# A fused attention, dense, SwiGLU and adapter kernel: SyncE's and GpSimd's orders in the first group, repeated waits of ScalarE, and the order at the end of attention

## The chip, the cores and the metric

One NeuronCore of one Trainium2 chip runs one program. The metric is the time of an execution on the device, in microseconds. The kernel before took 1306.64 us (median of three runs, 1304.0 to 1306.82).

## What is computed

Four residual steps on x, of shape [8, 128, 512] in float32:

```python
x = x + attention(x, Wq, Wk, Wv, Wo, norms, k_cache[block_table], v_cache[block_table], seqlens)
x = x + (x @ W.T + b) + coeff[b] * (x @ (2*mask[b] - 1))      # dense, its weights differ by batch element
x = x + down(silu(gate(x)) * up(x))                            # with low-rank adapters chosen by index
x = x + x @ weight[ids[b]].T
```

Attention has 8 batch elements, 8 key heads with 4 query heads each, head size 128, and 640 keys for each query: 512 out of 16 cache pages and 128 new ones. Queries and keys pass an RMS norm and a rotation by position.

## The kernel before

TensorE multiplies every float32 pair in three passes: each operand is split into a high part (a rounded copy, made by ScalarE) and a low part (the difference, made by GpSimd or VectorE), and `three_pass` (L65 to L67) issues high by high, high by low and low by high.

The work of attention is ordered as 8 groups (one per key head, `g`) of 8 rounds (one per batch element, `b`). Groups 1 to 6 are one loop on each engine; group 0, group 7 and `ending` (the last two rounds) are written out. Each engine's order within a round is written by hand, and semaphores carry all dependences. In round b an engine works on three elements at once: b (probabilities turned and multiplied with the values), the next one `(g1, b1)` (scores, softmax) and the one after that `(g2, b2)` (projection, rotation). A pass over one element goes so:

- TensorE projects the queries; VectorE multiplies them with cosines and sines (`turn_q`); GpSimd combines the halves (`rotate_q`, L568 and L569); VectorE transposes 32 by 32 squares (`spread_queries`, L1114); SyncE writes them to a scratch tensor in HBM with four DMAs (`store_queries`, L415, tensor `q_rows`) and reads them back transposed with one (`read_queries`, L421, tile `at_qT_raw`), a round later.
- ScalarE makes their high part (`queries`, tile `ds_lo`, L758) and GpSimd their low part (`queries`, L618). TensorE then forms the scores of four heads, VectorE masks them and takes the maximum (`mask_and_max`, L1073), ScalarE exponentiates (`exps`, L810), VectorE inverts the row sums (L1079, L1083), and GpSimd multiplies (`normalise`, L628).
- Three of the five chunks of probabilities are turned on TensorE (L1353); the other two go through HBM (`store_turned`, L402, then `read_turned`, L408, four DMAs, tensor `turned_rows`).

The cache has to be brought into page order for each key head. In group 0 the keys of elements 0 to 3 and all values come by row gathers that GpSimd issues (`gather`, L524). Meanwhile the pages of the next group are copied through one staging tile, `kv_stage`: GpSimd gathers 1 MB into it (`stage_pages`, L556, one step in each of four rounds), SyncE waits for that (`kv_staged`) and stores it in HBM (`store_pages`, L397, `kT_pages` and `v_pages`). GpSimd's next step waits for that store (`kv_stored`). `load_keys` (L379) and `load_values` (L385) read the pages of an element two rounds ahead.

In group 0, SyncE's round is: `read_queries`, `load_keys` where due, `store_turned`, `read_turned`, `load_x`, `store_queries`, and last `store_pages(g, b - 2)` in rounds 2 to 5. In groups 1 to 6, `store_pages(g, b - 2)` stands behind `store_turned` instead, and the steps are staged a round earlier (rounds 1 to 4), so that a step is stored a round after it is staged.

GpSimd's round in group 0 is: the row gathers for b2, `cached_keys` (L613), `queries` (L618), `rotate_q`, `key_scale`, `cached_values` (L624), the staging step, `normalise` of head 0, `query_scale` (L583, L585), `normalise` of the other heads, `rotate_k`, and `table(b + 3)` (L593).

In `ending`, the dense weights of batch elements 1 to 3 are formed on VectorE (`dense.weights`, L1564) and split (`part_hi`, L1590, ScalarE; `part_lo`, L1595, GpSimd) between the steps of the last two attention rounds. y is element 6 and z is element 7.

Of the kernel before, what the change touches and what calls it, by code (L numbers as in the profile page):

```python
# [84 lines left out]
def attention(nc, block, x, xT, ints, floats, wq, wkv, wo, k_cache, kT_cache, v_cache, kT_pages, v_pages, ident, xres, wq_raw, shared, dense, loads, turned_rows, q_rows):  # L85
# [3 lines left out]
    with ExitStack() as ctx:  # L89
# [250 lines left out]
        def _(sp):  # L340
# [89 lines left out]
            def group(g, last):  # L430
                for b in range(B):
# [17 lines left out]
                    if not (last and b >= B - 2) and not by_row(g2):  # L449
# [4 lines left out]
                    if by_moves(g, b):  # L454
                        store_turned(g, b)
                    if not by_row(g) and not last and 2 <= b < 6:
                        store_pages(g, b - 2)
                    if not (last and b >= B - 2) and not by_row(g2):
                        wait_apart(sp, v_cache_done, upto(g, b, 1, 1), passed)
                        load_values(g2, b2)  # L460
# [17 lines left out]
                    if by_row(g) and b < B - 2:  # L478
                        sp.wait_ge(xT_done, b + 3)
                        load_x(b + 2)  # L480
# [4 lines left out]
                    if by_row(g):  # L485
                        if b == 0:
                            store_first_keys(0)
                        elif 2 <= b < 6:
                            store_pages(g, b - 2)
                    elif not last and b == 0:  # L490
# [22 lines left out]
        def _(pool):  # L513
# [141 lines left out]
            def group(g, first, last):  # L655
                for b in range(B - 2 if last else B):
# [13 lines left out]
                    if b == B - 3 and not last:  # L670
                        qkv_group(g + 1, DC)
                    if keys_by_row(g2, b2):
# [5 lines left out]
                    if started:  # L678
                        if not keys_by_row(g1, b1):
                            cached_keys(g1, b1)  # L680
                        queries(g1, b1)
                    rotate_q(g2, b2)
                    if started:
                        key_scale(g2, b2)
                        cached_values(g1, b1)
                        stage()
                    else:
                        rotate_k(g2, b2)
# [8 lines left out]
                    if first and b == 1:  # L697
                        stage_first_keys(1)
                    normalise(g1, b1, 0)
                    if started:  # L700
# [3 lines left out]
                    if started:  # L704
                        rotate_k(g2, b2)
                    if first and b < B - 3:
                        table(b + 3)
                    if not started:
                        query_scale(g2, b2)
# [37 lines left out]
        def _(act):  # L747
# [12 lines left out]
            def qkv_group(g, n, first=False):  # L760
                cs = slice(2 * (n - DC), 2 * (n - DC) + 2)
                out, src = (wqT_hi[:, n, :], wq_raw[:, n, :]) if n < DC else (wkvT_hi[:, cs, :], wkv_raw[:, cs, :])
                if not first:
                    act.wait_ge(q_in_psum if n < DC else kv_in_psum, g * B)
                if first and n < DC:
                    hi(out, src, (wq_half_loaded, staging_loaded)[n // 2], 16, wq_hi_done)
                else:
# [1718 lines left out]
```

## Time and profile before

| | |
|---|---|
| median of three runs | 1306.64 us |
| the profiled execution's own time | 1306.46 us |
| its span, first to last instruction | 1304.5 us |
| TensorE busy | 1274.6 us (98%), mean granted clock 0.996 |
| VectorE busy | 1015.0 us (78%) |
| GpSimd busy | 931.9 us (71%) |
| ScalarE busy | 840.0 us (64%) |

PE is TensorE's matmuls, PEld its weight loads, DVE VectorE, ACT ScalarE, POOL GpSimd, SP SyncE, whose row "SPq" is the issuing of a DMA. In a timeline a row is one or several like instructions with start, duration, what it writes and reads, and in brackets the idle time before it with what ended it. A wait is counted only where the engine was idle. A row of windows gives the stretch, its length, the busy time (and number of instructions) of PE, PEld, DVE, ACT and POOL, the granted clock as a share of 2.4 GHz, the busy share of the DMA engines and GB/s. A row of waits gives who waited, for whom, the total, the number of times and the longest. Matmuls overlap their neighbours, so that busy TensorE time is not time at full rate. Group 0 lasts to about 174 us, and attention to about 1047 us.

### The profile page before, as it was taken

To read this page: it belongs to the slowest core of one execution; us is meant where nothing else is said; L and a number is where in the kernel's file an instruction comes from. 1 tells how busy PE (TensorE), PEld (TensorE's weight loads), DVE (VectorE), ACT (ScalarE), POOL (GpSimd) and SP (SyncE) were. 2 spreads that over 40 slices of the span, in tenths; PEclk is the share of its full clock that TensorE was granted. 3 is DMA by queue.
4 is the path that set the end of the run, shared out by engine and by line. 5 is a ranking of instruction groups with operands and counts; after the bars stand their busy time and mean duration, and the time that the engine had idled before them with its cause. 6 is when DMAs were issued, how large, how long until landed. Compare 5 with 4: busy or idle time off the path is not lost.

```text
span 1304.5 us, 25321 instructions
## 1 busy us (share of the span) xinstructions
PE 1274.6 (98%) x7068; PEld 1112.4 (85%) x7068; DVE 1015.0 (78%) x2054; ACT 840.0 (64%) x2217; POOL 931.9 (71%) x1173
## 2 busy tenths in 40 slices
PE   9898999999999999999999999999999899999999
PEld 8777888888888888888888888888888788888887
DVE  6876788887887888788877887888888896748546
ACT  7665666766675767666766676676766684545444
POOL 7888887878887888787888888888887732414111
PEclk9999999999999999999999999999999999999999
DMA  6787769957985797689769966995756364354532
GB/s 224 234 243 233 208 202 275 268 142 206 275 248 161 219 284 215 176 234 278 198 177 263 259 174 181 287 274 147 232 156 170 120 193 142 131 197 135 182 127 80
DMA packets 260052, 265.86 MB, mean 204 GB/s; under 512 B 139776, under 2 KB 211072, under 8 KB 249216
## 3 DMA queue, kind: packets, MB, share of 16 engines
q1 hardware_dynamic: 254208, 228.77, 61.1%
q0 software_dynamic: 5760, 36.18, 8.2%
q8 instruction: 28, 0.46, 0.1%
q14 instruction: 56, 0.46, 0.1%
HBM read 182.57 MB, written 82.31 MB: 203 GB/s over the span
## 4 chain that ended last, share of the span: by engine, by line
PE 79%; POOL 5%; DMA 4%; DVE 4%; issue 4%; ACT 3%; SPq 1%; ACTq 0%; DVEq 0%; POOLq 0%
PE ps L65 24%; PE ps L66 23%; PE ps L67 23%; PE ps L1353 5%; DVE at_pT_lo L1021 1%; DMA shared<-in_kT_cache,at_page_idx 1%; DMA turned_rows<-at_turned 1%; DMA q_rows<-at_q_turned_rows 1%; POOL ds_lo L618 1%; POOL at_probs L628 1%; ACT at_probs L810 1%; PE ps L2308 1%; DVE xres L1090 1%; DMA at_qT_raw<-q_rows 1%; POOL at_q_rot L569 0%
## 5 line engine op out<-in xcount | busy, mean ns | idle before, releaser
L810 ACT ACTIVATE at_probs<-at_probs,at_neg_max 128x640 f32<-128x640 f32 x256 | 210.2, 823 | 122.2 <-DVE at_neg_max L1073 122.2
L628 POOL TENSOR_SCALAR at_probs<-at_probs,at_row_inv 128x640 f32<-128x640 f32 x256 | 212.9, 842 | 103.0 <-DVE at_row_inv L1083 99.5
L1073 DVE CUSTOM_DVE_ANT_0 at_probs<-ps,at_mask,at_inv_rms 128x640 f32<-128x640 f32 x256 | 223.4, 880 | 19.7 <-PE ps L67 17.3
L65 PE MATMUL ps<-ds_hi,x_hi 128*128 128x512 f32 (+1 forms) x564 | 192.8, 342 | 0.8 <-DVE x_lo L1614 0.4
L67 PE MATMUL ps<-ds_hi,x_lo 128*128 128x512 f32 (+1 forms) x564 | 192.2, 341 | 0.0
L65 PE MATMUL ps<-at_kT_hi,ds_lo 128*128 128x320 f32 x512 | 161.6, 316 | 11.4 <-DVE at_pT_lo L1021 8.5
L67 PE MATMUL ps<-at_kT_hi,ds_lo 128*128 128x320 f32 x512 | 159.7, 312 | 0.0
L66 PE MATMUL ps<-at_kT_lo,ds_lo 128*128 128x320 f32 x512 | 159.7, 312 | 0.0
L758 ACT ACTIVATE at_pT_hi<-ps 128x512 fp32r<-128x512 f32 x196 | 111.4, 604 | 69.0 <-PE ps L1353 64.6
L1021 DVE TENSOR_TENSOR at_pT_lo<-ps,at_pT_hi 128x512 fp32r<-128x512 f32 x196 | 128.5, 683 | 29.1 <-ACT at_pT_hi L758 28.4
L65 PE MATMUL ps<-at_pT_hi,at_v_hi 128*128 128x512 f32 x320 | 128.1, 400 | 8.2 <-DVE xres L1090 6.3
L66 PE MATMUL ps<-at_pT_lo,at_v_hi 128*128 128x512 f32 x320 | 126.1, 394 | 0.0
L67 PE MATMUL ps<-at_pT_hi,at_v_lo 128*128 128x512 f32 x320 | 125.0, 391 | 0.0
L1108 DVE STREAM_TRANSPOSE at_turned<-at_probs 128x768 f32<-128x768 f32 x62 | 60.7, 978 | 81.9 <-POOL at_probs L628 81.9
L66 PE MATMUL ps<-ds_lo,x_hi 128*128 128x512 f32 x308 | 120.1, 390 | 0.0
L65 PEld LDWEIGHTS ps<-ds_hi,x_hi 128*128 128x128 f32 x564 | 105.9, 188 | 16.2 <-issue 0.9
L67 PEld LDWEIGHTS ps<-ds_hi,x_lo 128*128 128x128 f32 x564 | 106.9, 190 | 12.3
L65 PEld LDWEIGHTS ps<-at_kT_hi,ds_lo 128*128 128x128 f32 x512 | 97.5, 190 | 22.9 <-DVE at_pT_lo L1021 12.6
L758 ACT ACTIVATE at_pT_hi<-at_pT_raw 128x512 fp32r<-128x512 f32 x124 | 74.9, 625 | 52.7 <-DMA at_pT_raw<-turned_rows 30.3
L65 PE MATMUL ps<-at_woT_hi,at_oT_hi 128*128 128x512 f32 x256 | 106.5, 416 | 0.0
L66 PEld LDWEIGHTS ps<-at_kT_lo,ds_lo 128*128 128x128 f32 x512 | 97.5, 190 | 4.1
L67 PE MATMUL ps<-at_woT_hi,at_oT_lo 128*128 128x512 f32 x256 | 100.7, 393 | 0.0
(226 smaller groups left out, 3624.1 us busy)
## 6 DMA issues: line engine op xcount, KB each, us to landing
turned_rows<-at_turned SPq DMA_DIRECT2D x62, 512.0 KB, 2.8
at_pT_raw<-turned_rows SPq DMA_DIRECT2D x248, 128.0 KB, 4.7
kT_pages<-shared SPq DMA_DIRECT2D x16, 1024.0 KB, 5.6
q_rows<-at_q_turned_rows SPq DMA_DIRECT2D x248, 64.0 KB, 2.9
at_qT_raw<-q_rows SPq DMA_DIRECT2D x62, 256.0 KB, 3.5
kv_raw<-kT_pages SPq DMA_DIRECT2D x60, 256.0 KB, 4.1
v_pages<-shared SPq DMA_DIRECT2D x14, 1024.0 KB, 5.7
kv_raw<-v_pages SPq DMA_DIRECT2D x56, 256.0 KB, 3.4
```

The costliest lines, as they stand in the source:

```text
L65: pe.matmul(out, l_hi, r_hi, start=first, stop=False)
L66: pe.matmul(out, l_hi, r_lo, start=False, stop=False)
L67: return pe.matmul(out, l_lo, r_hi, start=False, stop=last)
L618: pool.tensor_tensor(l, qT_raw[:].rearrange("p a h r -> p h a r"), h.bitcast(F32), ALU.subtract).then_inc(qT_done, 1)
L628: pool.tensor_scalar(probs[:, h, :], probs[:, h, :], row_inv[:, h:h + 1], 1.0, ALU.mult, ALU.mult).then_inc(probs_done, 1)
L758: act.activation(out, src, ACT.Copy).then_inc(done, 1)
L810: act.activation(probs[:, h, :], probs[:, h, :], ACT.Exp, bias=neg_max[:, h:h + 1], scale=-1.0, accum_out=row_sum[:, h:h + 1]).then_inc(ex ...
L1021: dve.tensor_tensor(out, src, hi_part.bitcast(F32), ALU.subtract).then_inc(done, 1)
L1073: dve.tensor_tensor_reduce(out=probs[:, h, :], in0=slot(h), in1=mask[:, b, :], scale=inv_rms[b % 2][:, h:h + 1], scalar=3.0e38, op0=ALU.ad ...
L1090: dve.tensor_tensor(xres[:, b, :], bank(y_bank(b)), xres[:, b, :], ALU.add).then_inc(dense.x1_ready if last else y_added, 1)
L1108: dve.transpose(turned[:, :, :, 0:n, :].rearrange("p k c h r -> p h c k r"), probs[:, 0:n, (KC - MOVED) * P:KEYS].rearrange("p h (c k i) - ...
L1353: return pe.transpose(bank(probs_bank(b, c))[:, h * S:(h + 1) * S], probs[:, h, c * P:(c + 1) * P], ident[:])
```

## The change

It reorders and removes; no arithmetic is changed.

- SyncE, group 0: `store_pages` stands behind `store_turned` and runs in rounds 3 to 6; `load_x` stands behind `store_queries`; the first load of keys and values of group 1 waits for the last page store behind `store_queries` of round 6.
- GpSimd: the row gathers and the staging step stand behind the low parts and `rotate_q`; in the round before `ending`, `query_scale` stands behind the other heads' `normalise` and `rotate_k`; in round 0 of group 0, `query_scale` stands before `table`.
- ScalarE: waits that an earlier wait of the engine already covers are taken out (`pv_done` before the high parts of the values, and the second to fourth wait of each group of weights).
- `ending`: `dense.weights(2, ...)` and the matching `part_hi` stand later, among the steps of the last round.

SyncE:

```diff
+                    stored_last = by_row(g) and b2 == 0
-                    if not (last and b >= B - 2) and not by_row(g2):
+                    if not (last and b >= B - 2) and not by_row(g2) and not stored_last:
...
                     if by_moves(g, b):
                         store_turned(g, b)
+                    if by_row(g) and 3 <= b < 7:
+                        store_pages(g, b - 3)
...
-                    if by_row(g) and b < B - 2:
-                        sp.wait_ge(xT_done, b + 3)
-                        load_x(b + 2)
...
                     if not (last and b >= B - 2):
                         store_queries(g2, b2)
-                    if by_row(g):
-                        if b == 0:
-                            store_first_keys(0)
-                        elif 2 <= b < 6:
-                            store_pages(g, b - 2)
-                    elif not last and b == 0:
+                    if by_row(g) and b < B - 2:
+                        sp.wait_ge(xT_done, b + 3)
+                        load_x(b + 2)
+                    if stored_last:
+                        sp.wait_ge(kv_stored, STAGED_FIRST + 64)
+                        sp.wait_ge(kc_done, b + 1)
+                        load_keys(g2, b2)
+                        sp.wait_ge(v_cache_done, b + 1)
+                        load_values(g2, b2)
+                    if by_row(g) and b == 0:
+                        store_first_keys(0)
+                    if not by_row(g) and not last and b == 0:
```

GpSimd:

```diff
+                    if started:
+                        if not keys_by_row(g1, b1):
+                            cached_keys(g1, b1)
+                        queries(g1, b1)
+                        rotate_q(g2, b2)
+                        key_scale(g2, b2)
+                        cached_values(g1, b1)
                     if keys_by_row(g2, b2):
                         pool.wait_ge(kc_in_psum, b + 1)
                         gather(b2, k_rows, k_raw, k_loaded)
...
                     if started:
-                        if not keys_by_row(g1, b1):
-                            cached_keys(g1, b1)
-                        queries(g1, b1)
-                    rotate_q(g2, b2)
-                    if started:
-                        key_scale(g2, b2)
-                        cached_values(g1, b1)
                         stage()
...
+                    before_ending = last and b == B - 3
                     normalise(g1, b1, 0)
-                    if started:
+                    if started and not before_ending:
                         query_scale(g2, b2)
                     for h in range(1, G):
                         normalise(g1, b1, h)
                     if started:
                         rotate_k(g2, b2)
+                    if before_ending or not started:
+                        query_scale(g2, b2)
                     if first and b < B - 3:
                         table(b + 3)
-                    if not started:
-                        query_scale(g2, b2)
```

ScalarE (`qkv_group` is cut in the same way as `wo_group`):

```diff
             def wo_group(g, n):
-                if not (isinstance(g, int) and g == 0):
-                    act.wait_ge(y_in_psum, g * B)
-                hi(woT_hi[:, n, :], wo_raw[:, n, :], staging_loaded, g * 32 + 32, wo_hi_done)
+                if n == 0:
+                    act.wait_ge(staging_loaded, g * 32 + 32)
+                    if not (isinstance(g, int) and g == 0):
+                        act.wait_ge(y_in_psum, g * B)
+                act.activation(woT_hi[:, n, :], wo_raw[:, n, :], ACT.Copy).then_inc(wo_hi_done, 1)
...
             def cached_values(g, b):
                 j = b % 2
-                if upto(0, b, 1) >= 2 or not (isinstance(g, int) and g == 0):
-                    act.wait_ge(pv_done, upto(g, b, KC) - KC - 1)
...
             def new_values(g, b):
-                if upto(0, b, 1) >= 2 or not (isinstance(g, int) and g == 0):
-                    act.wait_ge(pv_done, upto(g, b, KC) - KC)
```

`ending`, ScalarE and then VectorE:

```diff
-                for c in range(DC - 1):
-                    dense.part_hi(act, 2, c)
+                dense.part_hi(act, 2, 0)
+                dense.part_hi(act, 2, 1)
                 probs_T(g, z, 3)
                 probs_T(g, z, 4)
                 dense.x1_hi(act, 2, X1_BANK[2])
-                dense.part_hi(act, 2, DC - 1)
+                dense.part_hi(act, 2, 2)
+                dense.part_hi(act, 2, 3)
...
-                for c in range(DC - 1):
-                    dense.weights(dve, 2, c)
+                dense.weights(dve, 2, 0)
                 probs_T(g, z, 0)
                 probs_T(g, z, 1)
                 probs_T(g, z, 2)
+                dense.weights(dve, 2, 1)
                 dense.add(dve, 0)
-                dense.weights(dve, 2, DC - 1)
+                probs_T(g, z, 3)
                 add_y(g, y, True)
-                probs_T(g, z, 3)
                 probs_T(g, z, 4)
+                dense.weights(dve, 2, 2)
                 dense.x1_lo(dve, 2, X1_BANK[2])
+                dense.weights(dve, 2, 3)
```

## Rows read from the trace of the kernel before

**Rows 1.** Windows of group 0 and of group 1: busy time of each engine, granted clock, DMA.

```profile
51.05:142.43 91.38, 80.84 (x427) 69.64 (x426) 65.62 (x147) 57.09 (x159) 78.53 (x102) 0.94 0.80 236
...
142.43:158.27 15.84, 15.26 (x87) 12.93 (x86) 12.17 (x29) 9.27 (x29) 11.02 (x16) 1.00 0.75 195
174.07:296.20 122.13, 121.76 (x701) 107.98 (x700) 99.98 (x220) 82.97 (x239) 102.34 (x131) 1.00 0.80 227
```

**Rows 2.** Waits of TensorE, 50 to 150 us: total, times, longest.

```profile
PE ps L65 <- DVE at_pT_lo L1021: 8.0, 4, 3.7
```

**Rows 3.** Waits of ScalarE, 80 to 150 us.

```profile
ACT ds_lo L758 <- DMA at_qT_raw<-q_rows: 17.2, 4, 5.3
```

**Rows 4.** Timeline of SyncE's queue in group 0: start, duration.

```profile
82.39 0.36 SPq L397 DMA_DIRECT2D kT_pages<-shared  x1
82.80 0.43 SPq L421 DMA_DIRECT2D at_qT_raw<-q_rows  x1
...
93.90 2.16 SPq L415 DMA_DIRECT2D q_rows<-at_q_turned_rows  x4
```

**Rows 5.** Chain that ended last, in order of time, group 0.

```profile
84.23 7.39 DMA turned_rows<-at_turned
...
133.88 8.08 DMA q_rows<-at_q_turned_rows
```

**Rows 6.** Timeline of SyncE's queue in group 1.

```profile
205.42 0.36 SPq L397 DMA_DIRECT2D kT_pages<-shared  x1
...
210.13 1.74 SPq L415 DMA_DIRECT2D q_rows<-at_q_turned_rows  x4
215.85 0.34 SPq L421 DMA_DIRECT2D at_qT_raw<-q_rows  x1
```

**Rows 7.** Waits of GpSimd, 51 to 142 us.

```profile
POOL at_probs L628 <- DVE at_row_inv L1083: 6.4, 5, 2.3
POOL ds_lo L618 <- ACT ds_lo L758: 2.8, 3, 1.2
```

**Rows 8.** Timeline of GpSimd, group 0; in brackets idle time before.

```profile
102.66 1.41 POOL L593 TENSOR_TENSOR shared<-shared,at_floats 128x256 f32<-128x256 f32 x2
104.25 1.11 POOL L524 DMA_INDIRECT kv_raw<-in_L_cond_v_cache,at_key_idx  x1 [0.18 <-issue]
...
107.39 1.27 POOL L618 TENSOR_TENSOR ds_lo<-at_qT_raw,ds_lo 128x512 fp32r<-128x512 f32 x1 [0.72 <-ACT ds_lo L758]
...
112.88 1.09 POOL L556 DMA_INDIRECT shared<-in_kT_cache,at_page_idx  x1 [0.28 <-POOL at_page_idx L553]
115.08 0.80 POOL L628 TENSOR_SCALAR at_probs<-at_probs,at_row_inv 128x640 f32<-128x640 f32 x1 [1.11 <-DVE at_row_inv L1083]
```

**Rows 9.** Timeline of GpSimd, group 1.

```profile
211.82 1.08 POOL L556 DMA_INDIRECT shared<-in_L_cond_v_cache,at_page_idx  x1 [1.36 <-DMA kT_pages<-shared]
```

**Rows 10.** Waits of ScalarE, 175 to 1000 us.

```profile
ACT at_pT_hi L758 <- PE ps L1353: 63.1, 49, 1.5
...
ACT at_oT_hi L758 <- issue: 18.5, 5, 4.9
```

**Rows 11.** Timeline of GpSimd at the end of attention.

```profile
1008.12 1.34 POOL L585 TENSOR_TENSOR at_inv_rms<-at_inv_rms,at_minus_half 128x4 f32<-128x4 f32 x1
...
1013.53 1.32 POOL L618 TENSOR_TENSOR ds_lo<-at_qT_raw,ds_lo 128x512 fp32r<-128x512 f32 x1
```

**Rows 12.** Timeline of TensorE at the end of attention.

```profile
1013.36 0.30 PE L1329 MATMUL ps<-ident,at_k_rot 128*128 128x128 f32 x1 [0.95 <-DVE at_v_lo L1066]
...
1016.25 0.30 PE L65 MATMUL ps<-at_kT_hi,ds_lo 128*128 128x320 f32 x1
...
1037.33 0.50 PE L65 MATMUL ps<-at_pT_hi,at_v_hi 128*128 128x512 f32 x1 [1.59 <-DVE at_pT_lo L1021]
```

**Rows 13.** Timeline of VectorE at the end of attention.

```profile
1026.67 5.20 DVE L1564 SCALAR_TENSOR_TENSOR shared<-shared,ds_coeff,staging 128x512 f32<-128x512 int32 x3
...
1040.26 0.74 DVE L1564 SCALAR_TENSOR_TENSOR kv_raw<-kv_raw,ds_coeff,staging 128x512 f32<-128x512 int32 x1
```

More of the change, by code:

```diff
@@ L455, in group @@
                         store_turned(g, b)
+                    if by_row(g) and 3 <= b < 7:
+                        store_pages(g, b - 3)
                     if not by_row(g) and not last and 2 <= b < 6:
                         store_pages(g, b - 2)
-                    if not (last and b >= B - 2) and not by_row(g2):
+                    if not (last and b >= B - 2) and not by_row(g2) and not stored_last:
                         wait_apart(sp, v_cache_done, upto(g, b, 1, 1), passed)
@@ L678, in group @@
                     if started:
-                        if not keys_by_row(g1, b1):
-                            cached_keys(g1, b1)
-                        queries(g1, b1)
-                    rotate_q(g2, b2)
-                    if started:
-                        key_scale(g2, b2)
-                        cached_values(g1, b1)
                         stage()
                     else:
+                        rotate_q(g2, b2)
                         rotate_k(g2, b2)
@@ L762, in qkv_group @@
                 out, src = (wqT_hi[:, n, :], wq_raw[:, n, :]) if n < DC else (wkvT_hi[:, cs, :], wkv_raw[:, cs, :])
-                if not first:
-                    act.wait_ge(q_in_psum if n < DC else kv_in_psum, g * B)
                 if first and n < DC:
-                    hi(out, src, (wq_half_loaded, staging_loaded)[n // 2], 16, wq_hi_done)
-                else:
-                    hi(out, src, *((staging_loaded, g * 32 + 16, wq_hi_done) if n < DC else (wkv_loaded, g * 16 + 16, wkv_hi_done)))
-            def wo_group(g, n):
-                if not (isinstance(g, int) and g == 0):
-                    act.wait_ge(y_in_psum, g * B)
-                hi(woT_hi[:, n, :], wo_raw[:, n, :], staging_loaded, g * 32 + 32, wo_hi_done)
+                    act.wait_ge((wq_half_loaded, staging_loaded)[n // 2], 16)
+                elif n == DC:
+                    act.wait_ge(wkv_loaded, g * 16 + 16)
+                elif n == 0:
+                    act.wait_ge(staging_loaded, g * 32 + 16)
+                if not first and n in (0, DC):
+                    act.wait_ge(q_in_psum if n == 0 else kv_in_psum, g * B)
+                act.activation(out, src, ACT.Copy).then_inc(wq_hi_done if n < DC else wkv_hi_done, 1)
+            def wo_group(g, n):
+                if n == 0:
[3 more added lines that the diff above has]
+                act.activation(woT_hi[:, n, :], wo_raw[:, n, :], ACT.Copy).then_inc(wo_hi_done, 1)
             def cached_values(g, b):
                 j = b % 2
-                if upto(0, b, 1) >= 2 or not (isinstance(g, int) and g == 0):
-                    act.wait_ge(pv_done, upto(g, b, KC) - KC - 1)
                 if by_row(g):
```

## The prediction

> **What bounds the kernel now.** I read the page first: TensorE is busy 98% of the span and carries 79% of the chain that ended last, so only TensorE's idle or slowed time can be won. Then I cut the span into windows. In group 1 the eight rounds take 122.1 us, or 15.27 each, with TensorE busy throughout [rows 1]. In group 0, rounds 1 to 5 (from one start of GpSimd's round to the fifth after it) take 91.4 us, 15.0 more than five rounds of 15.27: TensorE lacks 10.5 us of busy time, and its granted clock averages 0.94, so that part of the busy time ran at 1.2 GHz after idle stretches. Round 6 takes 15.8, 0.6 over.
>
> Who is late there? TensorE waits for low parts of probabilities, 8.0 us in four waits [rows 2]. That is a wait inherited: ScalarE makes the high parts only behind the high part of the queries, and for these it waits 17.2 us in four waits, for the read of `at_qT_raw` [rows 3]. SyncE's queue says why the read is late: it is issued at 82.80, right behind a page store at 82.39 that had waited for the gather into `kv_stage` [rows 4]. The chain then shows what followed: the store of the turned probabilities took 7.39 us behind that 1 MB store, which pushed the next queries' stores to 93.90, and in the worst round their landing took 8.08 us [rows 4, 5]. So one wait of SyncE runs through three transfers into the next round.
>
> **SyncE's order (group 0).** Removed: the wait for a gather just issued. The page store moves to a place where its gather is a round old, so it waits for nothing. The read of the queries then follows the landing of their stores. `load_x`, one issue of about 0.4 us, leaves the path in front of these stores. Group 1 has exactly this order, and there the stores are issued from 210.13 to 211.87 and are read at 215.85 [rows 6], 4.0 us after the last, and its rounds run at full rate. I take the queries' wait as gone.
>
> What is late next is GpSimd, since nothing that it executes is removed. In the five rounds it waits 6.4 us for row sums and 2.8 us for ScalarE's queries [rows 7], 9.2 in all. That is the ceiling of the gain in rounds 1 to 5: its remaining work is 82.2 us against TensorE's 76.4.
>
> **GpSimd's order (group 0).** From the start of its low part of the queries (107.39) to its first `normalise` (115.08) pass 7.7 us, which is the way over TensorE, VectorE and ScalarE [rows 8]. In between it has work until 113.97, so it waits 1.1. The gather, 1.3 us with its gap, now lies within these 7.7 us and not ahead of them. The work in between becomes 7.9 us where the step has its index instructions and some 0.8 less where it has not. I estimate 1.1 us of waiting left in the five rounds, half a microsecond each in two of them. Gain: 9.2 - 1.1 = 8.1 us. In round 6 GpSimd has 11.0 us of work, TensorE is the bound again, and the 0.6 goes: 8.7 us in group 0. Bounds: 0 (the waits are replaced) and 9.8.
>
> Does the move add waits? The next staging step waits for the page store, now issued in the same round. In group 1 that costs GpSimd 1.36 us, until 6.4 us after the store's issue [rows 6, 9], and is hidden, because `normalise` waits anyway. In group 0 GpSimd has the table (1.41 us) and the gather (1.3) to do before it gets there [rows 8], so it comes 1.3 us after the landing. A landing up to 7.7 us costs nothing; beyond, each microsecond delays `normalise`, three times. The row gathers for b2 start some 6 us later in their round and are needed in the next: hidden. The turned reads now queue behind the page store, as in group 1, which runs without stall. The keys of group 1's first element wait for the last page store. The store is issued about 1 us behind that of the turned probabilities and lands 6.4 later, and with about 5 us for the load they are there 12.5 us into a round of 15.3; SyncE's next read of queries stands behind them but waits for its own stores that long.
>
> **ScalarE's waits.** Some 30 waits per pass of the loop go. ScalarE is idle before the high parts that feed TensorE 49 times, 63.1 us, on TensorE itself [rows 10]: that hides what they cost. One place is open: at the loop's back edge ScalarE issues nothing for up to 4.9 us, 18.5 in five [rows 10], and TensorE feels part of it. If a shorter body shortened that, a tenth of it would be 1.8 us. The rows give no reason that it should; I take 0, bounds -1.8 and 0.
>
> **Query scale before the end.** It takes 2.0 us (the power 1.34 of them [rows 11]) and stands ahead of three `normalise`. Moved behind, TensorE's idle 0.95 at 1013.36 [rows 12] can shrink by some 0.8, since the row sums come late as well. But the scale then stands ahead of the low part of z's queries. That ended at 1014.85 [rows 11], 1.4 before TensorE's scores at 1016.25 [rows 12]; it moves 2.0 later and 0.8 earlier, so to 1016.05. The scores start no more than 0.2 earlier. I take 0.1, bounds -0.2 (a loss) and 0.8. In round 0 `query_scale` and `table` swap, both in front of the same wait: 0.
>
> **Dense weights.** TensorE idles 1.59 us at 1037.33 for a low part [rows 12] that stood behind two weights of 1.7 us. With one of them behind, it starts about 1.9 us earlier. Behind it, weights (2, 2) and (2, 3) now precede VectorE's low part of the attended values, on which TensorE's last output waits, and that gives most of it back. A weight takes 1.73 us on average in the three at 1026.67, when GpSimd makes low parts, and 0.74 at 1040.26, when it does not [rows 13]. With both moved ones fast the output is 1.0 earlier, with both slow 0.1 earlier. I take 0.4, bounds -0.5 and 1.9. The GPSIMD Engine Reference of the Trainium skill (Specifications) says that GpSimd's SBUF interfaces are shared with VectorE and that they contend when a VectorE instruction has two SBUF inputs; the trace agrees, and by that rule alone both would be slow, for a sum 0.3 us smaller.
>
> **The sum.** 8.7 + 0 + 0.1 + 0.4 = 9.2 us. The profiled execution took 1306.46 us (span 1304.5 and 2.0 around it), so 1297.3; the median of the runs shown, 1306.64, is 0.2 above it. Everything after group 0 only shifts.
>
> **The rivals.**
> *A, the forecast:* 1297.3, own range 1295 to 1300. Chance 0.65.
> *B, the queries' stores stay slow:* the 8.08 us [rows 5] came not from SyncE's lateness but from the 1 MB gather in flight, which began before them. Then ScalarE would go on waiting, and only `load_x`, the gather's move and round 1 would help, about 3 us: 1303.5. Against it: in group 1 a gather also starts as the stores end (211.82) and they land in 4.0 us [rows 6, 9]; with the row gather ahead of it, the page gather now begins about 1.3 us behind the last store. Chance 0.15. DMA: Bandwidth & Descriptors of the Trainium skill (Issuing engines are not separate DMA queues) says that all engines' transfers run on the same 16 DMA engines and interleave; by that alone the order of issue would matter less than the load, as in B, and the rows of the two groups weigh against it.
> *C, slower:* the page store in front of the turned reads and of GpSimd's step lands late. Beyond 7.7 us each microsecond costs one in each of three rounds. The gain of 9.2 is eaten at 10.8 us of landing, the time then 1306.5, and at 11.8 us it would be 1309.5. The longest landing here is 8.08 us, of another tensor [rows 5]. Chance 0.05.
> *D, no change to speak of:* ScalarE's wait was cover for another that ends at the same time (the turned reads behind the page store), round by round: 1305.5. Chance 0.06.
> *E, more than A:* the back edge shrinks, the end gives its 1.9 and GpSimd's ceiling is reached: up to 13 us, 1293.5. Chance 0.09.
>
> **The numbers.** Range 1294.0 to 1303.5: A, most of E, and B up to its value; outside it lie C, D and half of B, about 0.2. A measurement of this kernel tells about 0.2%, or 2.6 us, from no change. Faster by more than that (under 1304.0): A, E and nearly all of B, 0.88. Within: D and the rest of B and some of C, 0.08. Slower: 0.04.
>
> **What would show it.** After: ScalarE's wait for `at_qT_raw` in group 0 falls from 17.2 to under 3 us; the six rounds from 51 to 158 us take about 98 us in place of 107; GpSimd is busy nearly without a gap in rounds 3 to 5, and TensorE's clock stays near 1.0 there. TensorE's waits turn into many short ones for GpSimd's or VectorE's results. Group 1's rounds stay at 15.27 and the back edge at 3.7 us in the mean. The idle 1.59 at the end is gone, and a wait for the attended values stands ahead of the last output. Wrong it would be if GpSimd waited for `kT_pages` or `v_pages` in group 0 (C), or if SyncE's read still came 6 us or more after the last of the four stores (B).

## The result, and the profile after

The changed kernel takes 1293.07 us in the median of 4 runs (1292.4 to 1294.06), the one before 1306.18 (1304.0 to 1306.82, 4 runs): ratio 0.9903, 95% interval 0.9886 to 0.992. The forecast of 1297.3 was 4.2 us too high, and the result lies below its range. The profiled execution has a span of 1291.2 us against 1304.5, so 13.3 less.

To see where it went I use one mark in every group: the start of one of VectorE's additions of an output to x (L1090 before, L1100 after). In groups 1 to 6 it is the addition of the sixth round, in group 7 that of the third. So mark 1 lies in group 1, ahead of the loop's first jump back; where an expectation speaks of the first output of the first group, it means this mark.

| mark in group | 1 | 2 | 3 | 4 | 5 | 6 | 7 | end of span |
|---|---|---|---|---|---|---|---|---|
| before, us | 257.37 | 383.00 | 507.38 | 631.50 | 755.64 | 879.85 | 957.04 | 1304.5 |
| after, us | 251.66 | 374.71 | 497.66 | 620.76 | 743.72 | 866.67 | 943.87 | 1291.2 |
| ahead by | 5.7 | 8.3 | 9.7 | 10.7 | 11.9 | 13.2 | 13.2 | 13.3 |

Group 1's own rounds kept their length, as the windows below show. So group 0 gave 5.7 us, the five back edges of the loop (the jumps from the end of a pass to its start) 2.6, 1.4, 1.0, 1.2 and 1.3, together 7.5, and what lies behind them 0.1. The 7.5 us come from the part that the forecast had at nothing.

The windows of the changed kernel, over the same work as [rows 1] (us, busy time of PE, PEld, DVE, ACT and POOL, granted clock, DMA share, GB/s):

```profile
51.19:138.37 87.18, 77.92 (x428) 65.67 (x428) 71.76 (x148) 57.94 (x160) 80.14 (x103) 1.00 0.79 242
138.37:153.14 14.77, 14.77 (x87) 13.20 (x87) 12.11 (x28) 9.47 (x30) 11.52 (x16) 1.00 0.83 232
168.42:290.55 122.13, 121.80 (x701) 108.04 (x700) 100.23 (x220) 83.43 (x241) 101.80 (x131) 1.00 0.81 229
```

Rounds 1 to 5 take 87.18 us in place of 91.38 [rows 1], at a clock of 1.00 in place of 0.94, and round 6 takes 14.77 in place of 15.84. Of the 4.2 us of rounds 1 to 5, 2.9 are the same matmuls run faster (TensorE's busy time falls from 80.84 to 77.92) and 1.3 are idle time (10.5 to 9.3): most of TensorE's idle time is still there, in shorter pieces. Group 1's eight rounds are what they were. Then the waits that answer to [rows 2, 3, 7], of TensorE (50 to 150 us), ScalarE (80 to 150) and GpSimd (51 to 138):

```profile
PE ps L1340 <- DVE at_v_lo L1076: 2.4, 2, 2.1
PE ps L65 <- DVE at_pT_lo L1031: 2.4, 2, 1.6
PE ps L65 <- DVE xres L1100: 1.8, 3, 1.1
PE ps L65 <- POOL ds_lo L624: 1.2, 1, 1.2
...
ACT ds_lo L766 <- DMA at_qT_raw<-q_rows: 5.5, 3, 3.4
...
POOL at_q_rot L574 <- DVE a_raw L1062: 1.3, 1, 1.3
POOL at_probs L634 <- DVE at_row_inv L1093: 0.9, 2, 0.7
POOL ds_lo L624 <- ACT ds_lo L766: 0.9, 1, 0.9
```

ScalarE's 17.2 us [rows 3] are 5.5, not the promised 3 or less. SyncE's queue shows what is left of them; it answers to [rows 4]:

```profile
74.18 2.79 SPq L415 DMA_DIRECT2D q_rows<-at_q_turned_rows  x4
77.02 0.49 SPq L348 DMA_DIRECT2D xres<-in_x  x1
82.72 0.34 SPq L421 DMA_DIRECT2D at_qT_raw<-q_rows  x1
...
91.48 2.56 SPq L415 DMA_DIRECT2D q_rows<-at_q_turned_rows  x4
94.08 0.45 SPq L348 DMA_DIRECT2D xres<-in_x  x1
97.08 0.34 SPq L421 DMA_DIRECT2D at_qT_raw<-q_rows  x1
```

No page store stands between the stores and the read any more, only `load_x` (0.5 us), and still the read comes 5.7 us after the issue of the last store in one round (76.97 to 82.72) and 3.0 in the next: that is the landing of the stores themselves, rival B, in one round of five. GpSimd's timeline answers to [rows 8]:

```profile
108.64 1.12 POOL L530 DMA_INDIRECT kv_raw<-in_L_cond_v_cache,at_key_idx  x1 [0.17 <-POOL at_v_lo L630]
109.80 0.77 POOL L557 TENSOR_SCALAR at_page_row<-at_page_row 128x1 f32<-128x1 f32 x1
110.63 0.19 POOL L559 CAST at_page_idx<-at_page_row 128x1 uint32<-128x1 f32 x1
111.09 1.04 POOL L562 DMA_INDIRECT shared<-in_kT_cache,at_page_idx  x1 [0.28 <-POOL at_page_idx L559]
112.16 1.82 POOL L634 TENSOR_SCALAR at_probs<-at_probs,at_row_inv 128x640 f32<-128x640 f32 x1
```

The wait of 1.11 ahead of `normalise` is gone, but the `normalise` now takes 1.82 us where it took 0.80, here and in one more of the five rounds (1.83 at 60.74). The gather in front of it suggests itself as the cause, but VectorE's timeline names another. The first row is of the changed kernel; the other three are of run h4 below, which has the same gather at the same place:

```profile
112.06 1.34 DVE L1031 TENSOR_TENSOR at_pT_lo<-at_pT_raw,at_pT_hi 128x512 fp32r<-128x512 f32 x2
```
```profile
108.69 1.04 POOL L562 DMA_INDIRECT shared<-in_kT_cache,at_page_idx  x1 [0.28 <-POOL at_page_idx L559]
109.76 0.82 POOL L634 TENSOR_SCALAR at_probs<-at_probs,at_row_inv 128x640 f32<-128x640 f32 x1
109.94 1.78 DVE L1029 TENSOR_TENSOR at_pT_lo<-at_pT_raw,at_pT_hi 128x512 fp32r<-128x512 f32 x2 [0.20 <-ACT at_pT_hi L764]
```

In the changed kernel VectorE had started two subtractions with both inputs in SBUF 0.1 us ahead of the `normalise`, which then took 1.0 us longer. In h4 the `normalise` came first by 0.2 us and took 0.82, right behind the gather, and VectorE's two took 1.78 in place of 1.34. In the kernel before, the wait for the row sums had let `normalise` (115.08) start 0.6 us ahead of the same subtractions. So the cost comes from meeting VectorE, and the wait had kept the two apart.

The back edge, in ScalarE's waits of 175 to 1000 us, against [rows 10]:

```profile
ACT at_probs L819 <- DVE at_neg_max L1083: 101.3, 47, 3.2
ACT at_pT_hi L766 <- PE ps L1364: 68.9, 51, 1.5
ACT at_oT_hi L766 <- PE ps L67: 36.5, 49, 1.0
```

"at_oT_hi <- issue" does not occur any more. The timeline of the first instruction of a pass, before at 299.62, after at 289.95:

```profile
299.62 0.60 ACT L758 ACTIVATE at_oT_hi<-ps 128x512 fp32r<-128x512 f32 x1 [4.92 <-issue]
```
```profile
289.95 0.60 ACT L766 ACTIVATE at_oT_hi<-ps 128x512 fp32r<-128x512 f32 x1 [0.95 <-PE ps L67]
```

And the queues by which instructions are loaded (packets, MB, share), of the kernel before, and of the one after:

```profile
q8 instruction: 28, 0.46, 0.1%
q14 instruction: 56, 0.46, 0.1%
```
```profile
q8 instruction: 28, 0.46, 0.2%
q14 instruction: 31, 0.25, 0.1%
```

q14 moved 25 packets fewer, five for each of the five back edges on average. Between 299 and 672 us the kernel before loads five packets in each of three passes, the changed one none; cut to 16 us around each back edge, the kernel before shows two every time.

### The profile page after: what moved, and what is told of

It is laid out like the page before. It is cut to its first block, busy times and chain, and to the rows that moved or that the text cites. A ratio compares the mean times of both kernels' runs of the same rounds, so it can differ in the third digit from the quotient of the medians.

```text
span 1291.2 us, 25180 instructions
## 1 busy us (share of the span) xinstructions
PE 1269.8 (98%) x7068; PEld 1110.1 (86%) x7068; DVE 1017.5 (79%) x2054; ACT 840.3 (65%) x2217; POOL 932.9 (72%) x1173
## 4 chain that ended last, share of the span: by engine, by line
PE 87%; DVE 6%; POOL 4%; ACT 1%; issue 1%; DMA 1%; SPq 0%; DVEq 0%; POOLq 0%; ACTq 0%
PE ps L65 26%; PE ps L66 25%; PE ps L67 25%; PE ps L1364 6%; DVE at_pT_lo L1031 2%; POOL at_probs L634 1%; PE ps L1406 1%; DVE ds_lo L1031 1%; DVE at_probs L1083 1%; PE ps L2319 1%; DMA q_rows<-at_q_turned_rows 0%; ACT at_pT_hi L766 0%; DVE xres L1100 0%; PE ps L1340 0%; POOL at_inv_rms L591 0%
## 5 line engine op out<-in xcount | busy, mean ns | idle before, releaser
L634 POOL TENSOR_SCALAR at_probs<-at_probs,at_row_inv 128x640 f32<-128x640 f32 x256 | 215.8, 853 | 104.3 <-DVE at_row_inv L1093 99.7
L1083 DVE CUSTOM_DVE_ANT_0 at_probs<-ps,at_mask,at_inv_rms 128x640 f32<-128x640 f32 x256 | 223.6, 880 | 19.5 <-PE ps L67 17.5
L65 PE MATMUL ps<-at_kT_hi,ds_lo 128*128 128x320 f32 x512 | 159.9, 312 | 4.7 <-DVE at_pT_lo L1031 1.3
L67 PE MATMUL ps<-at_kT_hi,ds_lo 128*128 128x320 f32 x512 | 158.1, 309 | 0.0
L65 PEld LDWEIGHTS ps<-ds_hi,x_hi 128*128 128x128 f32 x564 | 105.9, 188 | 16.7 <-issue 1.2
L67 PEld LDWEIGHTS ps<-ds_hi,x_lo 128*128 128x128 f32 x564 | 106.9, 189 | 12.3
L66 PE MATMUL ps<-at_woT_lo,at_oT_hi 128*128 128x512 f32 x256 | 100.5, 393 | 0.0
```

Of the source, the lines that this page charges most:

```text
L65: pe.matmul(out, l_hi, r_hi, start=first, stop=False)
L66: pe.matmul(out, l_hi, r_lo, start=False, stop=False)
L67: return pe.matmul(out, l_lo, r_hi, start=False, stop=last)
L634: pool.tensor_scalar(probs[:, h, :], probs[:, h, :], row_inv[:, h:h + 1], 1.0, ALU.mult, ALU.mult).then_inc(probs_done, 1)
L1083: dve.tensor_tensor_reduce(out=probs[:, h, :], in0=slot(h), in1=mask[:, b, :], scale=inv_rms[b % 2][:, h:h + 1], scalar=3.0e38, op0=ALU.ad ...
```

## The experiments

Two theories stood first. **S:** ScalarE stops at the back edge because code has to be loaded, and the shorter pass does without. **G:** the loop only inherits a better state from group 0. Each kernel was timed beside the one before on its chip, and the ratio is against that; marks are read in the profiled executions. The mark of group 1 came at 250.9 to 252.3 in the nine profiled executions with the changed kernel's group 0, and at 257.0 to 258.9 in the four with that of before, so a difference below 2 us there says little.

**One part alone.** e1: ScalarE's waits only (`qkv_group`, `wo_group`, `cached_values`, `new_values` as changed). e2: SyncE's and GpSimd's order of group 0. e3: the end. e4: all but ScalarE's waits.

> The kernel before with ScalarE's waits alone taken out. Theory S (the loop's back edge: ScalarE's body is short enough to start its next pass without a stop): the 4.9 us in which ScalarE issues nothing ahead of the first at_oT_hi of a pass are gone, groups 1 to 6 take some 7.5 us less, the first group changes by under 0.5; about 1298.7. Theory G (the whole gain comes from the first group's order, and the loop gains by what it inherits from it, such as transfers in flight): no change, 1306, back edge still 3 to 5 us.

> The kernel before with SyncE's and GpSimd's order of the first group alone. Theory S: 5.7 us less, all of it before the first output of the first group, 1300.5, and the back edge still stops ScalarE 3 to 5 us. Theory G: all or nearly all of the 13, 1293 to 1295.

> The kernel before with the query scale and the dense weights of the end alone. Both theories: 0 to 0.5 us less, 1305.7 to 1306.2. If the parts did not add up, this is where more than 1 us would have to be.

> The changed kernel with ScalarE's waits put back. Theory S: 1300.6 us, 7.5 more than the changed kernel, the stop of 3 to 5 us back at each of the five back edges. Theory G: 1293, as the changed kernel.

| kernel | median us, ratio (95%) | mark of group 1 | mark 1 to mark 6 | mark 7 to end | at_oT_hi <- issue |
|---|---|---|---|---|---|
| before | | 257.37 | 622.48 | 347.46 | 18.5 |
| after | 1293.07, 0.9903 (0.9886 to 0.992) | 251.66 | 615.01 | 347.33 | none |
| e1, waits | 1300.6, 0.9946 (0.9926 to 0.9966) | 258.88 | 617.22 | 347.60 | none |
| e2, group 0 | 1299.93, 0.994 (0.9923 to 0.9958) | 252.23 | 622.53 | 348.34 | 18.5 |
| e3, end | 1305.78, 0.998 (0.9966 to 0.9993) | 257.44 | 623.58 | 345.70 | 18.4 |
| e4, all but waits | 1297.94, 0.9931 (0.9912 to 0.9949) | 251.08 | 620.50 | 345.74 | 16.7 |

S holds and G falls: with the waits taken out the stop is gone in e1 and the loop is shorter (617.22, of which one late round near 811 us, 17.43 in place of 15.28, is 2.2), and with them in it is there in e2, e3 and e4, whatever group 0 does. Against the changed kernel the four later back edges cost 1.0 to 1.4 us each, before and in e4; the first costs 2.6 in the kernel before and 1.0 in e4, which is why e4 is 5.5 and not 7.5 above the changed kernel in this column. The medians support the signs, not these sizes: the three parts alone are 7.1, 7.8 and 2.6 us below the kernel before, 17.5 together, and the whole change is 12.7 below it here and 16.2 in c1 on another chip. The end surprised: alone it gives 1.8 us, and in the changed kernel 0.1. Windows of the changed kernel and of e4 over the same work show where that went:

```profile
997.00:1000.00 3.00, 1.44 (x10) 0.81 (x8) 2.39 (x5) 2.92 (x7) 2.92 (x6) 0.98 0.09 34
1000.00:1002.00 2.00, 2.00 (x6) 1.61 (x6) 1.77 (x4) 1.69 (x4) 2.00 (x3) 0.50 0.52 211
1002.00:1004.00 2.00, 2.00 (x7) 1.58 (x7) 0.00 (x0) 0.12 (x1) 2.00 (x3) 0.68 0.55 166
```
```profile
1002.00:1005.00 3.00, 1.46 (x9) 0.93 (x9) 2.50 (x5) 2.82 (x7) 2.92 (x7) 1.00 0.13 51
1005.00:1007.00 2.00, 2.00 (x11) 1.62 (x10) 1.57 (x4) 1.80 (x4) 2.00 (x2) 1.00 0.46 186
1007.00:1009.00 2.00, 2.00 (x15) 1.74 (x14) 0.83 (x2) 0.00 (x0) 2.00 (x3) 1.00 0.59 181
```

After three microseconds in which TensorE was busy for half the time, its clock fell to 0.50 (the lower of its two levels) in the changed kernel for some 3 us, which costs the 1.6 us between 347.33 and 345.74; in e4, equally idle there, it stayed at 1.00. Of the twelve profiled executions with this end the clock fell there in four (the changed kernel, c1, h1, h2), and these have 347.2 to 347.7 from mark 7 to the end; the other eight have 345.6 to 345.9.

**Count, place or the waits themselves?** A shorter pass can help in three ways: by fewer instructions (N), by fewer waits (W), or because it lies at another place in the program (P). In the compiled programs, counted by instructions, ScalarE's pass of the loop has 391 instructions before and stands at 342 to 732 of its program; after, 371 at 331 to 701. An increment of a semaphore that nobody waits for moves this without adding a wait. The edit, in ScalarE's `group`, ahead of `exps(g1, b1, 0)`:

```
+                    if by_row(g):               # f1: 5, f3: 18, h1: 16, h2: 2 in b < 7
+                        pads(5)                 # act.sem_inc(passed, 1), 5 times
                     exps(g1, b1, 0)
```

f2 has `pads(2 + b % 2)` where `g` is the loop's register, so inside the pass.

> The changed kernel with 40 increments of a semaphore that nobody waits for, 5 in each round of the first group, in ScalarE's straight code ahead of the loop. Counting instructions in the compiled program, ScalarE's pass of the loop then runs from 371 to 741 instead of 331 to 701; its length stays at 371. In the kernel before it ran from 342 to 732, 391 long. Theory P (place: the stop comes when the end of the pass lies beyond some place between 701 and 732, because the start of the pass is then no longer at hand): the stops of 3 to 5 us are back at all five back edges, 1298.5 to 1300.5. Theory N (number of instructions in the pass) and theory W (the waits themselves): no stops, 1293.

> The changed kernel with 20 increments of a semaphore inside ScalarE's pass of the loop, so that it has the 391 instructions of the kernel before, but runs from 331 to 721. Theory N: stops back, 1298.5 to 1300.5. Theory W: no stops, 1293. Theory P doesn't decide: the end lies between the place that stopped and the one that did not, and the run tells on which side.

> The kernel before, all its waits in place, with 144 increments of a semaphore more, 18 in each round of the first group, ahead of the loop in ScalarE's code. The pass then runs from 486 to 876. Theory P, if the code comes in blocks of 256: start and end lie in fewer blocks again, the stops are gone although the kernel only got longer, about 1299 to 1300 (the first group may lose up to 1). Theories N and W: stops as before, 1306 to 1307.

f1 brought the stop back with a pass not an instruction longer and no wait added (17.6 us in five, q14 56 packets, median 1298.57), so neither the count alone (N) nor the waits (W) make it. f2, whose pass ends at 721, stops too (17.1, 1297.38). But f3 refuted P with blocks of 256. A pass that ends at 701 does not stop and one from the same start that ends at 721 does, so a block would have to end between the two. The pass from 486 to 876 would then touch one block fewer and run through, and it still stops (17.6; 1307.7, ratio 0.9999, 0.9983 to 1.0015). Another size of the blocks fitted all five programs: q14's packets are 8 KB, 0.25 MB in 31, and an instruction of the compiled program has 64 bytes, so a packet holds 128 of them. That is theory Q, with three predictions of its own.

> The changed kernel with 128 increments of a semaphore ahead of the loop in ScalarE's code, 16 in each round of the first group: the pass runs from 459 to 829, still 371 long. Theory Q (the code comes in blocks of 128 instructions, and the start of a pass is still at hand at its end only if the pass lies in three blocks): stops with the pass at 342 to 732, 371 to 741, 331 to 721 and 486 to 876, and none at 331 to 701, fit it, if the last lies within the first 14 places of a block; a shift by a whole block then keeps it so: no stops, 1293 to 1294. Theory L (a limit that the end of the pass must not cross, or simply less code ahead of it is better): the stops are back, 1298 to 1299.

> The changed kernel with 14 increments ahead of the loop, 2 in each of the first seven rounds: the pass runs from 345 to 715. Theory Q: 371 instructions fit into three blocks of 128 from 14 places out of 128 only, so a shift by 14 must bring the stops back wherever in them the pass stood, 1297.5 to 1299. Theory L: undecided, its limit lies between 701 and 721.

> The changed kernel with 64 increments ahead of the loop in VectorE's code, 8 in each round of the first group: VectorE's pass of 328 instructions runs from 410 to 737 instead of 346 to 673. Theory Q, if it holds for VectorE with blocks at about the same places: it then lies in four blocks, VectorE stops some 3.5 us at each of the five back edges, and TensorE, which needs VectorE's low parts within 1 to 2 us, loses 1.5 to 3 of them each time: 1300 to 1308. A theory of something peculiar to ScalarE: 1293.

| kernel | ScalarE's pass | median us, ratio (95%) | mark 1 to mark 6 | stop, us in five | q14 packets |
|---|---|---|---|---|---|
| after | 331 to 701 | 1293.07 | 615.01 | none | 31 |
| h1, 128 ahead | 459 to 829 | 1292.96, 0.9887 (0.987 to 0.9903) | 615.19 | none | 32 |
| h2, 14 ahead | 345 to 715 | 1299.93, 0.9938 (0.9922 to 0.9955) | 622.81 | 18.7 | 56 |
| f1, 40 ahead | 371 to 741 | 1298.57, 0.9929 (0.9903 to 0.9955) | 621.42 | 17.6 | 56 |
| f2, 20 inside | 331 to 721 | 1297.38, 0.9922 (0.9895 to 0.9949) | 621.47 | 17.1 | 56 |
| f3, before, 144 ahead | 486 to 876 | 1307.7, 0.9999 (0.9983 to 1.0015) | 621.41 | 17.6 | 57 |
| h3, VectorE | 331 to 701 | 1301.47, 0.9961 (0.9949 to 0.9974) | 625.04 | 12.4, VectorE's | 57 |

All three came as Q says: a shift by 128 does nothing, a shift by 14 costs 7 to 8 us, and a shift of VectorE's own pass by 64 makes VectorE stop. (h4 and i2 below shift VectorE's pass by 15, from 346 to 361; it does not stop, which Q allows.) The first two rows are h3's waits of 175 to 1000 us, the last is h2's ScalarE at a back edge:

```profile
DVE at_oT_lo L1031 <- issue: 12.4, 5, 2.6
...
PE ps L1343 <- DVE at_v_lo L1076: 8.1, 5, 1.8
```
```profile
292.43 0.60 ACT L770 ACTIVATE at_oT_hi<-ps 128x512 fp32r<-128x512 f32 x1 [3.81 <-issue]
```

**Group 0.** Why 5.7 and not 8.7? g1 has SyncE's order alone, g2 GpSimd's alone, h4 moves the tables:

```
-                    if first and b < B - 3:     # GpSimd's group
-                        table(b + 3)
...
                     inverse(g1, b1, 3)          # VectorE's group
+                    if first and b < B - 3:
+                        table(b + 3)
                     turn_first_heads(g1, b1, G - 1)
```

and i1 puts `stage()` of group 0 behind the last `normalise` of the round; i2 is i1 and h4 together; c1 is the changed kernel once more, on their chip.

> The kernel before with SyncE's order of the first group alone (GpSimd, ScalarE and the end untouched). By my forecast the late read of the queries is the cause and falls away: ScalarE's wait for them goes from 17 to under 4 us, and 3 to 4.5 of the 5.1 to 6.3 us that both orders gave together come from here; 1302 to 1303.5. Rival: the gather on GpSimd ahead of its low part is what holds TensorE, and this alone gives under 1.5: 1305 to 1306.

> The kernel before with GpSimd's order of the first group alone. SyncE's order alone moved the first output of the first group 4.2 us forward, both together 5.1 to 6.3. Theory U (the late read of the queries holds the rounds, and GpSimd's order only shortens what is left once it is gone): this alone gives 0 to 1 us there. Theory V (each order takes its own share): 1 to 2.5 us. Forecast of the text was that SyncE's wait is the root, so U; 1305 to 1307.

> The changed kernel with the tables of the first group's rounds (two multiplications, 1.41 us on GpSimd in each of five rounds) made by VectorE, just before it waits for GpSimd's normalised probabilities. If GpSimd's work is what sets the first group's rounds of 17 us now, as its row of gapless work says: each of five rounds 0.8 to 1.3 us shorter, 1287 to 1289, the lowest of all. Rival: VectorE, 84% busy there, takes over as the bound and nothing is won, 1291 to 1294.

> The changed kernel with the page gather of the first group's rounds behind the last normalise of its round and not ahead of the first. In the changed kernel the normalise behind a gather takes 1.8 us in place of 0.8. Theory C (GpSimd's sum of work sets the rounds; the gather and the microsecond after it cost the same wherever they stand): the rounds stay at 17.0, the slow instruction is now rotate_k or the one behind it, 1292 to 1294. Theory D (it is the place: 1.1 + 0.3 + 1.0 us between VectorE's row sums and the probabilities that TensorE waits for): three of the rounds shorten by 0.5 to 1.5 us, 1289 to 1291.

> The changed kernel with both: the tables made by VectorE, and the page gather behind the last normalise. With the tables away GpSimd waited again (1.0 and 1.7 us for ScalarE's queries), so its sum of work no longer sets every round, and the place of the gather can count. Theory D: 0.5 to 2 us below the kernel with the tables alone moved (1289.9), 1288 to 1289. Theory C: the same as that one, or slower by up to 1 where the later gather delays the low part of the keys.

> The changed kernel once more, beside the others on one chip, so that versions within 4 us of it can be told apart: 1293.1 as before, all theories; the profile says how much its first group and its end move from execution to execution.

| kernel | median us, ratio (95%) | mark of group 1 |
|---|---|---|
| g1, SyncE's order | 1301.87, 0.9951 (0.9937 to 0.9966) | 253.18 |
| g2, GpSimd's order | 1310.65, 1.0011 (0.9999 to 1.0022) | 262.91 |
| h4, tables on VectorE | 1289.86, 0.9862 (0.9844 to 0.9881) | 247.67 |
| i1, gather late | 1303.75, 0.9962 (0.9948 to 0.9977) | 262.90 |
| i2, both | 1300.8, 0.9943 (0.9929 to 0.9957) | 259.38 |
| c1, changed | 1292.76, 0.9876 (0.9861 to 0.9891) | 251.26 |

SyncE's order is the root, as forecast: 4.2 us of 5.7, and ScalarE's wait for the queries is 1.6 us there. GpSimd's order alone is not neutral as I expected: its mark lies 5.5 us later than that of the kernel before in this execution. Its median has the same sign, but not outside the noise (the interval holds 1), and one of its ten executions took 1794.65 us, for which nothing here shows a cause. h4 did what it should: with 1.41 us of tables off GpSimd per round the mark comes 4.0 us earlier (3.6 against c1), so GpSimd's work did set the rounds. One of the two slow `normalise` is fast again there (0.82 us). h4 is the fastest kernel of all. On its chip it stands at 0.9862 of the kernel before and the changed kernel at 0.9876 on another, and these intervals overlap. But h1, which is the changed kernel with 128 increments that cost nothing, ran on h4's chip: 1292.47 to 1294.17 us in four executions, against 1287.5 to 1291.38 for h4. The spans of the profiled executions agree (1287.9 against 1291.2 and 1292.2).

i1 and i2 refuted both theories they were made for: 11.6 us lost at the mark against c1, and 11.7 against h4. Both theories took the gather for what slowed `normalise`; in i1 the instruction behind the gather (L569) takes its usual 0.33 us. SyncE's queue and GpSimd's gathers of i1 tell why:

```profile
84.42 0.32 SPq L402 DMA_DIRECT2D turned_rows<-at_turned  x1
91.35 0.34 SPq L397 DMA_DIRECT2D kT_pages<-shared  x1
91.73 3.00 SPq L408 DMA_DIRECT2D at_pT_raw<-turned_rows  x4
```
```profile
84.52 1.10 POOL L562 DMA_INDIRECT shared<-in_kT_cache,at_page_idx  x1 [0.28 <-POOL at_page_idx L559]
```

The page store of the next round waits for this gather, issued 6.8 us ahead of it, and the turned reads stand behind the store: 91.73 where the changed kernel has 89.16. ScalarE waits 14.8 us for them, in four waits up to 175 us. It is the wait that the change took out, put back at another transfer. g2 is the same thing again: its gather starts at 95.95, and with SyncE's old order the store waits for it until 103.52 and the read of the queries until 103.92.

## Why the prediction was wrong

**The step that failed** is "If a shorter body shortened that, a tenth of it would be 1.8 us. The rows give no reason that it should; I take 0, bounds -1.8 and 0." It measured 7.5 us in the profiled execution (5.5 against e4). Two things were wrong in it. The tenth was too small: stops of 16.7 to 18.5 us cost 5.5 to 7.5, three to four tenths. Of this the trace of the kernel before puts down 1.64 us of TensorE's idle time at the first back edge to a late low part, and 0.5 at each to a late addition; where the rest of each 1.0 to 1.4 us goes is not shown. And the trace did give a reason. A stop put down to "issue" in front of the first instruction of a pass [rows 10], with packets of q14 around it each time, is code loading, and the runs show that it depends on how many instructions a pass has and where it lies. That is a switch, 0 or all, and not a term with a small size; I should have carried "the stop falls away" as a rival of its own, about 7 us below the forecast. Rival E held the mechanism and 1293.5, but priced the back edge at 1.8 and needed everything else at its ceiling; that its number lies 0.4 us from the measured one is luck.

Had the section Instruction fetch mechanics in Runtime: NRT & Kernel Launch of the Trainium skill been weighed, it would have said so: a taken branch whose target is outside the window of two 256-instruction pages forces a fetch before execution can go on. The trace agrees that there is such a stop (3.2 to 4.9 us a pass), and the runs that it depends on place. They disagree on the size of the pieces. With two pages of 256 a pass of 371 that runs without a stop from 331 and from 459, and stops from 345, puts the end of a page between 701 and 721; a pass from 486 to 876 then lies in two pages and would not stop, and f3's does.

**Group 0, forecast 8.7, measured 5.7.** The mechanism was right (ScalarE's wait for the queries, the clock back at 1.00, GpSimd next in line), the size was not. GpSimd's waits of rounds 1 to 5 went from 9.2 us to 3.1 and not to 1.1: VectorE's `a_raw` (1.3) and one more wait for the queries (0.9) were not on my list, the second by rival B, whose slow landing stayed in one round. And GpSimd's busy time rose from 78.53 to 80.14, for the most part by the two `normalise` that met VectorE's subtractions. That makes 2.0 + 1.6 = 3.6 us, against 3.9 that rounds 1 to 5 fell short of the 8.1. Round 6 gave 1.1 in place of 0.6. The bounds of 0 and 9.8 held.

**The end, forecast 0.5.** Without a fall of the clock it gives 1.8 (e3, mark 7 to end: 347.46 to 345.70): 0.4 from the query scale, forecast 0.1, and 1.4 from the weights, forecast 0.4, both within their bounds. The promised wait for the attended values is there, 0.29 us, and the idle 1.59 us [rows 12] is gone. In the changed kernel's profiled execution the clock took 1.6 of it back, a term that the sum had no place for.

**C and D** are refuted: in group 0 GpSimd waits nowhere for `kT_pages` or `v_pages`, and no wait of the same size held the rounds in place of ScalarE's (ScalarE does wait longer for VectorE's maxima, 12.3 us in place of 4.5 between 80 and 150 us, but the rounds got shorter). Group 1's rounds stayed at 15.27 as promised; that the back edge would stay did not.

The sum as it came out is 5.7 + 7.5 + 0.1 = 13.3. With the back edge at its forecast, 1306.46 - 5.8 would have been 1300.7, inside the range: two errors with opposite signs, 3.0 and 7.5 us, of which the larger put the time outside. That the forecast missed by no more than 4.2 us is luck: the two partly cancel.

## What to carry to other kernels

When an engine's first instruction of a loop pass waits for "issue", look at the instruction queue's packets at that place, and treat the pass length and the place in the program as a switch: count the instructions of the pass, and after any edit to straight code ahead of the loop look at the back edge again, since here 14 instructions that do nothing cost 7 us and 128 cost none. When a wait is taken away, the instruction behind it starts at another moment of its neighbours' work: look at what they run then, since here a `normalise` that started 0.1 us behind VectorE's subtractions, and no longer ahead of them, took 1.0 us more. A queue that works in order passes a wait on to whatever stands behind it; a transfer may only be moved if its producer is still a round old at the new place.

## What the runs showed of the hardware

- In these kernels an engine that jumps back in its loop stops 3.2 to 4.9 us (ScalarE) or 2.4 to 2.6 us (VectorE) at some lengths and places of the pass and not at others. The ten positions tried fit pieces of 128 instructions of which a pass may touch three: 371 instructions did not stop at 331 and 459, and stopped at 345 and 371; 391 stopped at 331, 342 and 486; VectorE's 328 did not at 346 and 361 and did at 410. When it stops, about five packets of 8 KB are loaded per pass. Where in a piece the programs begin is not known. Pieces of 256 do not fit f3; pieces of 64 or 32 (six or twelve kept) fit ScalarE's positions but not VectorE's; other sizes are excluded only so far as these positions do it.
- A GpSimd `normalise` (128x640, in SBUF) that starts while VectorE subtracts with both inputs in SBUF takes longer by about what VectorE still has to do: 1.82 us for 0.80 with 1.2 us left, 1.31 with 0.7 left (132.26 in the changed kernel), 1.16 with 0.5 left (136.58 before). The gather in front is not the cause: the same `normalise` right behind a page gather took 0.82 in h4 and 0.81 in the kernel before (230.06), with VectorE's subtraction starting after it. No run moved VectorE's instruction by itself.
- At the end of attention, behind three microseconds in which TensorE was busy for about half the time, its clock stood at the lower level for some 3 us in four of twelve profiled executions, and stayed at the upper one in the other eight. What decides between the two stays open.
- One late round appears in five of the profiled executions: 17.43 us in place of 15.28 in e1, 16.78 in e3, 16.8 in h4, 16.6 in c1 and 16.1 in i2, and not in that of the changed kernel, which has c1's code. It is always the third round of group 6. ScalarE waits there 2.3 to 3.7 us for the read of the turned probabilities, against 1.4 in the changed kernel, and TensorE then 0.5 to 1.9 for VectorE's low part. Why this read lands late was not found.
